# Eight sums of weight blocks from VectorE to GpSimd, the splits and gates around them reordered, and A_down by SP's plain DMAs, in a LoRA feed-forward kernel

## The chip, the cores and the metric

The kernel runs on one core of one Trainium2 chip. The metric is the device time of one execution in microseconds; several executions are timed and the median is given. All data are float32; products run on TensorE as sums of float32r parts, a high part and the remainder.

## What is computed

64 sequences of 32 rows by 512 features. Each sequence has an adapter (for the low-rank terms) and a condition (for a 32 x 32 mixing matrix).

```python
gate = x @ W_gate.T + 0.5 * (x @ A_gate[a].T) @ B_gate[a].T     # 512 -> 1376
up   = x @ W_up.T   + 0.5 * (x @ A_up[a].T)   @ B_up[a].T
act  = silu(gate) * up
h    = x + act @ W_down.T + 0.5 * (act @ A_down[a].T) @ B_down[a].T
out  = h + einsum('bct,bcd->bdt', h, W[cond])                   # mixing within a sequence
```

## The kernel before

**Tiles.** Four sequences make a tile of 128 rows; there are 16 tiles. The first stage works on pairs of tiles (8 pairs, 0 to 7, t = 0 or 1 in a pair), the down stage on one tile after the other. The 1376 features are three sections of 352, 512 and 512 columns; a unit is a section of a tile, counted k = 0 to 5 in a pair, (s, t) = (0,0), (0,1), (1,0), (1,1), (2,0), (2,1).

**Splitting.** Every float32 operand of TensorE is split: ScalarE copies it to float32r (`hi`, L500), then VectorE subtracts that from the original (`lo`, L763). B of the low-rank terms is one instruction of each (L500, L767). A product is three matmuls per slice: hi by hi, hi by lo, lo by hi.

**Fast form.** Pairs 0 and 1 are plain. From pair 2 on (`fast_pair`), the part with sections 1 and 2 is computed with seven block products and not eight, p1 to p7, as in Strassen's scheme. It needs sums of blocks of x (`sum_x`, `split_s`) and sums of weight blocks, once, for gate and up: t3 = b22 - b12, t1 = b12 - b11, t2 = b22 - t1, t4 = b21 - t2, each 128 x 1024 (`sum_weights`, L801, on VectorE during pair 1). The sums t1, t2 and t4 are written over raw weights in the landing area, which is also where the split forms of t2, t1 and t4 will lie; so each split may overwrite what another has still to read, and the waits on `w_ready` (pieces and forms whose low part is done) and `weights_summed` (sums done) in `split_forms` guard that. `t3_raw` lies under `s_hi`. The splits of these forms stand in the queues of ScalarE and VectorE by hand, in the order of `SPLITS`.

**Order on TensorE in a fast pair.** `base(pr, 0)`, `lora(pr-1, 5)`, `base(pr, 1)` with `lora(pr, 0)` in it, p1 (b11), `lora(pr, 1)`, p7 (t3; in pair 2 after p2), p2 (b21), p6 (t2), p5 (t1), p4 (t4), p3 (b22), each for gate and up. `base(pr, k)` waits until the units that used its bank are gated: in fast pairs `act_ready` must have reached 6 (pr - 1) + 4 + k. The count `act_ready` goes up when VectorE has multiplied silu(gate) by up (`gate`, L872); `turn` transposes the result to a staging area (L880), and `spill` on SP sends that to `actT_dram`, from where `load_actT` brings it back for the down stage.

**Down stage.** A tile takes 11 chunks of W_down (`down_chunks`, L1300), with the columns of A_down of the tile's adapters beside them in `wd`, so that the low-rank t comes out of the same matmuls. Within the chunks of tile m, TensorE also does `down_lora` and `mix` of tile m - 1. ScalarE and VectorE split A_down (`split_a_dn`), the activations (`split_actT`), B_down, the mixing matrix (`split_mix`) and h (`residual_h`, `split_h`) of the neighbouring tiles. GpSimd gathers B (gate and up) by indirect DMA with the row numbers of the list `rows` (L441), and in the down stage the rows of A_down (four gathers a tile), B_down and the mixing matrix. SP gathers A of gate and up with plain DMAs whose row number is loaded from `rows` into a register (`first_row`, L389).

Each queue is in order; what stands behind a waiting instruction waits too.

## Time and profile before

| | us |
|---|---|
| time, median of 3 runs | 457.99 (457.64 to 458.76) |
| the profiled execution | 457.48 |
| its span in the trace | 455.6 |
| TensorE (PE) busy | 437.4 |
| VectorE (DVE) busy | 335.0 |
| ScalarE (ACT) busy | 213.3 |
| GpSimd (POOL) busy | 168.2 |

Times in the trace count from the start of the span. The profiled execution is 1.9 us longer than its span, and 0.5 us below the median. Lines are those of the kernel before; L500, L763 and L441 are helpers that many steps share, so a step is known by its operands. In the timelines, one matmul's duration overlaps the next one's: the rate is read from the starts.

### The profile page before, as it was taken

Reading aid. Unit: us, or ns where it says so; the run is one execution under the profiler, and the core shown is the slowest. Engines: PE = TensorE matmul, PEld = TensorE weight load, DVE = VectorE, ACT = ScalarE, POOL = GpSimd, SP = SyncE. Lnnn points to the kernel's source line nnn. Section 1 sums busy time; section 2 is a strip of 40 time slices with the busy share of each in tenths; the row PEclk is TensorE's granted clock in tenths of the full one; section 3 lists DMA queues with packets and bytes.
Section 4 is the critical chain, followed back from the end, with each engine's and each line's share of the span. In section 5 each row is a group of like instructions: output and inputs, shape, how many; then the busy total and the mean of one; then the engine's idle time right before and its main releaser. Section 6 shows DMA issues by size and latency. Waiting matters only on the chain.

```text
span 455.6 us, 7248 instructions
## 1 busy us (share of the span) xinstructions
PE 437.4 (96%) x2465; PEld 393.9 (86%) x2465; DVE 335.0 (74%) x621; ACT 213.3 (47%) x396; POOL 168.2 (37%) x156
## 2 busy tenths in 40 slices
PE   5999999977999999999999999988999999999997
PEld 4978988865898888888888888988999999999996
DVE  6778698876876866967867857976766676676665
ACT  6664334365436335444444444925434545433441
POOL 3612120120311211111111551675566676665630
PEclk9999999999899999999999999999999999999999
DMA  8965663325667467466475589787556666555631
GB/s 268 378 221 150 182 181 108 104 81 147 167 170 210 109 163 193 112 199 157 112 205 148 141 260 337 196 201 201 170 173 192 205 199 202 176 175 175 201 104 46
DMA packets 99699, 81.12 MB, mean 178 GB/s; under 512 B 50928, under 2 KB 83056, under 8 KB 99664
## 3 DMA queue, kind: packets, MB, share of 16 engines
q1 hardware_dynamic: 88368, 47.27, 37.1%
q0 software_dynamic: 11008, 33.30, 24.0%
q8 instruction: 19, 0.31, 0.3%
q10 hardware_dynamic: 288, 0.10, 0.1%
q14 instruction: 16, 0.13, 0.1%
HBM read 65.18 MB, written 15.47 MB: 177 GB/s over the span
## 4 chain that ended last, share of the span: by engine, by line
PE 86%; DVE 7%; DMA 2%; ACT 2%; issue 1%; SPq 1%; DVEq 0%; ACTq 0%
PE bank L1300 24%; PE bank L1146 9%; PE bank L1147 9%; PE bank L1148 8%; PE bank L1191 8%; PE bank L1192 8%; PE bank L1193 8%; PE bank L1214 4%; PE bank L1213 4%; PE bank L1330 2%; DVE wd L763 2%; DMA actT_raw<-actT_dram 2%; PE bank L1310 1%; DVE b_gu L767 1%; PE bank L1315 1%
## 5 line engine op out<-in xcount | busy, mean ns | idle before, releaser
L441 POOL DMA_INDIRECT b_raw<-in_b_rows,rows x48 | 50.8, 1059 | 199.3 <-DVE b_gu L767 198.7
L1300 PE MATMUL bank<-wd,actT_hi 128*128 128x288 f32 x648 | 112.0, 295 | 3.1 <-DVE actT_lo L763 1.9
L1300 PEld LDWEIGHTS bank<-wd,actT_hi 128*128 128x128 f32 x648 | 95.5, 188 | 4.7 <-issue 3.5
L441 POOL DMA_INDIRECT a_dn_raw<-in_a_dn_rows,rows x64 | 75.5, 1180 | 19.5 <-issue 19.5
L767 DVE SCALAR_TENSOR_TENSOR b_gu<-b_raw,low_rows,b_gu 128x1024 fp32r<-128x1024 f32 (+1 forms) x48 | 55.6, 1159 | 30.6 <-ACT b_gu L500 30.6
L1300 PE MATMUL bank<-wd,actT_lo 128*128 128x288 f32 (+1 forms) x324 | 69.4, 296 | 0.0
L1300 PEld LDWEIGHTS bank<-wd,actT_lo 128*128 128x128 f32 (+1 forms) x324 | 51.9, 188 | 0.0
L500 ACT ACTIVATE b_gu<-b_raw 128x1024 fp32r<-128x1024 f32 (+1 forms) x48 | 46.2, 963 | 12.2 <-DMA b_raw<-in_b_rows,rows 10.7
L585 ACT ACTIVATE act<-bank 128x512 f32<-128x512 f32 (+1 forms) x48 | 26.2, 547 | 44.1 <-PE bank L1214 43.9
L763 DVE TENSOR_TENSOR actT_lo<-actT_raw,actT_hi 128x1280 fp32r<-128x1280 f32 (+1 forms) x32 | 27.0, 885 | 15.5 <-ACT actT_hi L500 14.6
L872 DVE TENSOR_TENSOR act<-act,bank 128x512 f32<-128x512 f32 (+1 forms) x48 | 29.9, 622 | 8.1 <-PE bank L1214 7.3
L1213 PE MATMUL bank<-b_gu,tT_hi 128*128 128x512 f32 (+1 forms) x96 | 35.5, 370 | 0.0
L1214 PE MATMUL bank<-b_gu,tT_lo 128*128 128x512 f32 (+1 forms) x96 | 35.5, 370 | 0.0
L880 DVE STREAM_TRANSPOSE staging<-act 128x512 f32<-128x512 f32 (+1 forms) x48 | 31.4, 654 | 3.4
L500 ACT ACTIVATE tdT_hi<-tdT_raw 128x128 fp32r<-128x128 f32 x16 | 5.0, 311 | 60.2 <-DVE tdT_raw L1050 60.2
L1146 PE MATMUL bank<-w_gate_hi,xT_hi 128*128 128x480 f32 (+2 forms) x72 | 27.0, 375 | 5.5 <-DVE w_gate_lo L763 5.5
L441 POOL DMA_INDIRECT b_dn_raw<-in_b_dn_rows,rows x16 | 18.0, 1125 | 36.7 <-PE bank L1300 26.6
L1147 PE MATMUL bank<-w_gate_lo,xT_hi 128*128 128x480 f32 (+2 forms) x72 | 26.7, 371 | 0.0
L1148 PE MATMUL bank<-w_gate_hi,xT_lo 128*128 128x480 f32 (+2 forms) x72 | 26.7, 370 | 0.0
L500 ACT ACTIVATE actT_hi<-actT_raw 128x1280 fp32r<-128x1280 f32 (+1 forms) x32 | 23.3, 775 | 2.9 <-DMA actT_raw<-actT_dram 2.9
L1146 PEld LDWEIGHTS bank<-w_gate_hi,xT_hi 128*128 128x128 f32 x72 | 14.0, 195 | 8.3 <-issue 5.2
L1146 PE MATMUL bank<-w_up_hi,xT_hi 128*128 128x352 f32 x64 | 21.2, 331 | 0.0
(177 smaller groups left out, 993.8 us busy)
## 6 DMA issues: line engine op xcount, KB each, us to landing
actT_raw<-actT_dram SPq DMA_DIRECT2D x16, 640.0 KB
actT_dram<-staging SPq DMA_DIRECT2D x64, 128.0 KB, 2.8
x_sb<-in_x SPq DMA_DIRECT2D x16, 256.0 KB, 2.9
xT_raw<-in_xT SPq DMA_DIRECT2D x15, 256.0 KB, 3.0
out<-out_sb SPq DMA_DIRECT2D x15, 256.0 KB, 2.0
a_raw<-in_a_gu_rows SPq DMA_DIRECT2D x56, 64.0 KB, 2.4
actT_dram<-staging SPq DMA_DIRECT2D x32, 88.0 KB, 3.1
wd_raw<-in_w_down SPq DMA_DIRECT2D x10, 256.0 KB, 7.1
```

Of the source, the lines that this page charges most:

```text
L441: return pool.indirect_dma_start(dst, None, src, bass.IndirectOffsetOnAxis(ap=rows[:, tile, col:col + 1], axis=0))
L500: return nc.scalar.activation(dst, src, ACT.Copy)
L767: return nc.vector.scalar_tensor_tensor(b, raw, low_rows[:, :], b.bitcast(F32), ALU.mult, ALU.subtract)
L1146: pe.matmul(out_, x_hi, hi, start=(first and k == 0), stop=False)
L1147: pe.matmul(out_, x_hi, lo, start=False, stop=False)
L1148: last = pe.matmul(out_, x_lo, hi, start=False, stop=(stops and k == KH - 1))
L1191: pe.matmul(out_, xs[0], hi, start=(first and j == 0), stop=False, skip_group_check=True)
L1192: pe.matmul(out_, xs[0], lo, start=False, stop=False, skip_group_check=True)
L1193: last = pe.matmul(out_, xs[1], hi, start=False, stop=(j == 1), skip_group_check=True)
L1213: pe.matmul(out_, tT_hi[t][:, g, :], b, start=False, stop=False, skip_group_check=True)
L1214: pe.matmul(out_, tT_lo[t][:, g, :], b, start=False, stop=True, skip_group_check=True)\
L1300: last = pe.matmul(ps_down[e][half][:, 0:HALF], a[e][0:n, c, :], wd[0:n, c, part, at:at + HALF], start=(c == 0 and i == 0), stop=(c == NC ...
```

## The change

- `sum_weights` goes from VectorE to GpSimd: in pair 1 the eight sums stand between the gathers of B, four behind the gathers of section 1, two behind each of the first gathers of section 2.
- `SPLITS` becomes t2, t1, t4, t3. In the plain pair (pair 1), both engines split t2 later, behind B of section 2, then t1 gate, and at the pair's end, behind `split_x` (and on VectorE `sum_x`), t1 up, t4 gate and t4 up. t3 is split in pair 2 between `split_b(pr, 1, 0)` and `split_s`, which waits for it. TensorE's waits for t1 and t4 go, since p7 waits for the last form.
- In all fast pairs TensorE's waits for B stand between the product and the low-rank matmuls and not ahead of the product.
- In the last pair chunks 0 to 4 of W_down are split, in three places, and not 0 to 3 in one.
- In the down stage A_down of tiles 2 to 15 is loaded by SP with plain DMAs (`load_a_dn`), each behind the `load_actT` of the same tile; GpSimd keeps those of tiles 0 and 1. The loads for tile 2 stand ahead of `spill(7, 2)`.
- Tile 1 of the down stage: `split_a_dn(1)`, `split_actT(1)` and `mask_td(0)` stand ahead of the gates of units 4 and 5 of the last pair; TensorE begins it when units 0 to 3 are gated, with the high parts of three chunks, and does `mix(0)` behind nine chunks and not seven.

```diff
-SPLITS = [(f, m) for f in ("t2", "t3", "t1", "t4") for m in MATRICES]
+SPLITS = [(f, m) for f in ("t2", "t1", "t4", "t3") for m in MATRICES]
...
+            def load_a_dn(m):
+                reached(sp, a_dn_ready, m - 1)
+                for q in range(TILE_SEQS):
+                    sp.dma_start(a_dn_raw[m % 2][:, q, :],
+                                 a_dn_rows[bass.ds(first_row(m, TILE_SEQS + 1 + q), P), :])\
+                        .then_inc(a_dn_landed[m % 2], 16)
...
             sp.wait_ge(s_used, FAST)
             load_x(0, 0)
+            load_actT(2, 0)
+            load_a_dn(2)
             load_x(1, 1)
             spill(PAIRS - 1, 2)
-            load_actT(2, 0)
             load_actT(3, 1)
+            load_a_dn(3)
...
                 load_actT(2 * j + 2, 0)
+                load_a_dn(2 * j + 2)
...
                 load_actT(2 * j + 3, 1)
+                load_a_dn(2 * j + 3)
...
-                    gather(a_dn_raw[m % 2][:, q, :], a_dn_rows, m, TILE_SEQS + 1 + q).then_inc(a_dn_landed[m % 2], 16)
+                    gather(a_dn_raw[m][:, q, :], a_dn_rows, m, TILE_SEQS + 1 + q).then_inc(a_dn_first_landed[m], 16)
+
+            def sum_weights(f, i):
+
+                if f == "t3":
+                    pool.wait_ge(w_ready, GU_PIECES)
+                elif f != "t1":
+                    pool.wait_ge(weights_summed, 4 if f == "t2" else 6)
+                a, b = {"t3": ("b22", "b12"), "t1": ("b12", "b11"), "t2": ("b22", "t1"), "t4": ("b21", "t2")}[f]
+                m = MATRICES[i]
+                nc.gpsimd.tensor_tensor(block_raw(f, m), block_raw(a, m), block_raw(b, m), ALU.subtract)\
+                    .then_inc(weights_summed, 1)
+
+            def pair_with_sums(pr):
+                gather_b(pr, 1, 0)
+                gather_b(pr, 1, 1)
+                sum_weights("t3", 0)
+                sum_weights("t3", 1)
+                sum_weights("t1", 0)
+                sum_weights("t1", 1)
+                gather_b(pr, 2, 0)
+                sum_weights("t2", 0)
+                sum_weights("t2", 1)
+                gather_b(pr, 2, 1)
+                sum_weights("t4", 0)
+                sum_weights("t4", 1)
+                gather_b(pr + 1, 0, 0)
...
-            for pr in range(PAIRS):
+            pair(0)
+            pair_with_sums(1)
+            for pr in range(PLAIN, PAIRS):
                 pair(pr)
...
             gather_b_dn(0)
             for m in range(2, TILES):
-                gather_a_dn(m)
                 pool.wait_ge(down_done, m - 1)
                 gather_b_dn(m - 1)
                 gather_mix(m - 1)
...
                     if f == "t2":
                         sc.wait_ge(w_ready, GU_PIECES)
                         sc.wait_ge(weights_summed, 6)
-                    elif f == "t1":
-                        sc.wait_ge(w_ready, GU_PIECES + i)
-                        sc.wait_ge(weights_summed, 8)
                     elif f == "t3":
                         sc.wait_ge(xT_used[1], PLAIN)
-                    else:
+                    elif m == "up":
+                        sc.wait_ge(w_ready, GU_PIECES + i - (1 if f == "t1" else 0))
+                        sc.wait_ge(weights_summed, 8)
+                    elif f == "t4":
                         sc.wait_ge(w_ready, GU_PIECES + i)
                     hi(form_part(f, m, "hi"), block_raw(f, m)).then_inc(w_hi_ready, 1)
...
                 if isinstance(pr, int) and pr == PLAIN:
-                    sc.wait_ge(w_ready, GU_PIECES + 4)
+                    sc.wait_ge(w_ready, GU_PIECES + 8)
...
                 split_a(pr + 1, 0)
                 split_a(pr + 1, 1)
-                split_forms(0, 2)
                 silu(pr, 2)
                 split_b(pr, 2, 0)
+                split_forms(0, 2)
                 split_x(pr + 1, 0)
                 silu(pr, 3)
                 split_b(pr, 2, 1)
+                split_forms(2, 3)
                 split_x(pr + 1, 1)
+                split_forms(3, 6)
...
                 split_b(pr, 0, 1)
                 silu(pr, 0)
                 split_t(pr, 1)
-                if first:
-                    split_forms(2, 4)
                 copy_p1(pr)
                 split_b(pr, 1, 0)
                 silu(pr, 1)
                 if first:
+                    split_forms(6, 8)
                     split_s(pr)
-                    split_forms(4, 6)
                     silu(pr, 2)
+                    split_b(pr, 1, 1)
                     copy_p7(pr)
-                    split_forms(6, 8)
-                    split_b(pr, 1, 1)
                 else:
                     copy_p7(pr)
                     split_b(pr, 1, 1)
                     silu(pr, 2)
...
                     split_x(pr + 1, 0)
+                else:
+                    split_down(0, 3)
...
-                    split_down(0, 4)
+                    split_down(3, 5)
...
             split_a_dn(0, 0)
             sc.wait_ge(p5_done, 2 * FAST)
             split_actT(0, 0)
-            split_down(4, NC)
-            silu(PAIRS - 1, 4)
+            split_down(5, NC)
             split_a_dn(1, 1)
-            silu(PAIRS - 1, 5)
             sc.wait_ge(s_used, FAST)
             split_actT(1, 1)
+            silu(PAIRS - 1, 4)
+            silu(PAIRS - 1, 5)
             split_b_dn(0, 0)
             split_td(0)
             split_mix(0, 0)
+            split_h(0, 0)
             split_a_dn(2, 0)
-            split_h(0, 0)
             split_actT(2, 0)
             split_b_dn(1, 1)
...
-                sum_weights("t3")
                 gating(pr, 0)
                 split_b(pr, 1, 0)
-                sum_weights("t1")
                 gating(pr, 1)
                 split_b(pr, 1, 1)
-                sum_weights("t2")
                 split_a(pr + 1, 0)
                 split_a(pr + 1, 1)
-                split_forms(0, 2)
                 gating(pr, 2)
                 split_b(pr, 2, 0)
+                split_forms(0, 2)
                 split_x(pr + 1, 0)
                 gating(pr, 3)
-                sum_weights("t4")
                 split_b(pr, 2, 1)
+                split_forms(2, 3)
                 split_x(pr + 1, 1)
                 sum_x(pr + 1)
+                split_forms(3, 6)
...
                 split_b(pr, 0, 1)
-                if first:
-                    split_forms(2, 4)
                 split_b(pr, 1, 0)
                 if first:
+                    split_forms(6, 8)
                     split_s(pr)
                 gating(pr, 1)
-                if first:
-                    split_forms(4, 6)
-                else:
-                    split_b(pr, 1, 1)
+                split_b(pr, 1, 1)
                 gate(pr, 2)
+                if last:
+                    split_down(0, 1)
                 add_u3(pr, 0)
-                if not first:
-                    turn(pr, 2)
+                turn(pr, 2)
                 add_u3(pr, 1)
-                if first:
-                    turn(pr, 2)
-                    split_forms(6, 8)
-                    split_b(pr, 1, 1)
                 if not last:
                     split_x(pr + 1, 0)
+                else:
+                    split_down(1, 2)
                 add_u7(pr, 0)
+                if last:
+                    split_down(2, 3)
                 add_u7(pr, 1)
                 split_b(pr, 2, 0)
                 if not last:
                     split_a(pr + 1, 0)
                     split_a(pr + 1, 1)
                 else:
-                    split_down(0, 4)
+                    split_down(3, 5)
                 gating(pr, 3)
...
             split_a_dn(0, 0)
             split_actT(0, 0)
-            split_down(4, NC)
+            split_down(5, NC)
+            split_a_dn(1, 1)
+            split_actT(1, 1)
+            split_b_dn(0, 0)
+            mask_td(0, 0)
             gating(PAIRS - 1, 4)
-            split_a_dn(1, 1)
             gating(PAIRS - 1, 5)
-            split_actT(1, 1)
-            ve.wait_ge(s_used, FAST)
-            split_b_dn(0, 0)
-            down(1, 1)
+            split_mix(0, 0)
+            residual_h(0, 0)
+            split_a_dn(2, 0)
+            split_actT(2, 0)
+            split_b_dn(1, 1)
+            residual_out(0, 0)
...
                 for i, m in enumerate(MATRICES):
-                    pe.wait_ge(w_ready, GU_PIECES + 3 + i)
+                    pe.wait_ge(w_ready, GU_PIECES + 7 + i)
...
                     p7(pr)
-                pe.wait_ge(b_ready[0], NS * pr + 2)
                 for i, m in enumerate(MATRICES):
                     pe.wait_ge(p1_copied, fast(pr, i))
                     p2 = product(ps[m][0][:, :], xT_hi[0], xT_lo[0], 1, "b21", m, False)
                     if i:
                         p2.then_inc(xT_used[0], 1)
+                    else:
+                        pe.wait_ge(b_ready[0], NS * pr + 2)
                     lora_half(ps[m][0][:, :], 0, i, PIECE)
...
-                    pe.wait_ge(w_ready, GU_PIECES + 5 + i)
                     pe.wait_ge(u3_ready, fast(pr, i))
                     product(ps[m][3][:, :], s_hi[1], s_lo[1], 1, "t1", m, False).then_inc(p5_done, 1)
-                pe.wait_ge(b_ready[1], NS * pr + 2)
                 for i, m in enumerate(MATRICES):
-                    pe.wait_ge(w_ready, GU_PIECES + 7 + i)
                     p4 = product(ps[m][0][:, :], xT_hi[1], xT_lo[1], 1, "t4", m, False)
                     if i:
                         p4.then_inc(xT_used[1], 1)
+                    else:
+                        pe.wait_ge(b_ready[1], NS * pr + 2)
                     lora_half(ps[m][0][:, :], 1, i, PIECE)
...
-            def first_chunks(c1):
+            def first_chunks(m, e, c1):
+                pe.wait_ge(actT_hi_ready, m + 1)
                 for c in range(c1):
-                    pe.wait_ge(w_ready, DN_FIRST + c + 1)
+                    if m == 0:
+                        pe.wait_ge(w_ready, DN_FIRST + c + 1)
                     for part in range(2):
                         for half in range(2):
-                            at = half * HALF
-                            pe.matmul(ps_down[0][half][:, 0:HALF], actT_hi[0][:, c, :], wd[:, c, part, at:at + HALF],
+                            at = RR * e + half * HALF
+                            pe.matmul(ps_down[e][half][:, 0:HALF], actT_hi[e][:, c, :], wd[:, c, part, at:at + HALF],
                                       start=(c == 0 and part == 0), stop=False)
-                pe.wait_ge(actT_ready, 1)
+                pe.wait_ge(actT_ready, m + 1)
...
-            def down(m, e, first=False):
+            def down(m, e, early=False):
                 pe.wait_ge(a_dn_ready, m + 1)
-                if first:
-                    pe.wait_ge(actT_hi_ready, 1)
-                    first_chunks(3)
+                if early:
+                    first_chunks(m, e, 3)
                 else:
                     pe.wait_ge(actT_ready, m + 1)
                     reached(pe, h_ready, 2 * (m - 1))
                     down_chunks(m, e, 0, 3)
-                if not first:
+                if not isinstance(m, int) or m > 0:
                     down_lora(m - 1, 1 - e)
-                down_chunks(m, e, 3, 7)
-                if not first:
+                mix_at = 9 if early else 7
+                down_chunks(m, e, 3, mix_at)
+                if not isinstance(m, int) or m > 0:
                     reached(pe, out_ready, m - 1)
                     mix(m - 1)
-                down_chunks(m, e, 7, NC).then_inc(down_done, 1)
+                down_chunks(m, e, mix_at, NC).then_inc(down_done, 1)
 
             pe.wait_ge(act_ready, NU * (PAIRS - 1) + 2)
-            down(0, 0, first=True)
-            pe.wait_ge(act_ready, NU * PAIRS)
-            down(1, 1)
+            down(0, 0, early=True)
+            pe.wait_ge(act_ready, NU * (PAIRS - 1) + 4)
+            down(1, 1, early=True)
```

## Rows read from the trace of the kernel before

**Rows 1.** The page, part 1: busy us of each engine, share of the span, instructions.
```profile
PE 437.4 (96%) x2465; PEld 393.9 (86%) x2465; DVE 335.0 (74%) x621; ACT 213.3 (47%) x396; POOL 168.2 (37%) x156
```

**Rows 2.** Waits of TensorE over the span: waiter, releaser, us in total, times, longest.
```profile
PE bank L1191 <- DVE b_gu L767: 5.7, 2, 3.4
PE bank L1146 <- DVE w_gate_lo L763: 5.5, 2, 5.3
PE bank L1300 <- DVE actT_lo L763: 1.9, 1, 1.9
PE bank L1300 <- issue: 1.2, 1, 1.2
```

**Rows 3.** Timeline of TensorE, pair 2: start, duration, instruction, [idle time before, releaser].
```profile
87.37 0.38 PE L1146 MATMUL bank<-w_gate_hi,xT_hi 128*128 128x480 f32 x1
...
92.57 0.39 PE L1191 MATMUL bank<-b_gate_hi,xT_hi 128*128 128x512 f32 x1
...
98.44 0.50 PE L1191 MATMUL bank<-b_gate_hi,xT_hi 128*128 128x512 f32 x1 [2.31 <-DVE b_gu L767]
...
102.20 0.39 PE L1191 MATMUL bank<-t_gate_hi,s_hi 128*128 128x512 f32 x1
...
113.96 0.61 PE L1191 MATMUL bank<-t_gate_hi,xT_hi 128*128 128x512 f32 x1 [3.43 <-DVE b_gu L767]
...
119.33 0.40 PE L1191 MATMUL bank<-b_gate_hi,s_hi 128*128 128x512 f32 x1
```

**Rows 4.** Timeline of VectorE, pairs 1 and 2, same columns.
```profile
56.91 2.35 DVE L801 TENSOR_TENSOR t_raw<-gu_landing 128x1024 f32<-128x1024 f32 x2
...
81.96 0.69 DVE L763 TENSOR_TENSOR xT_lo<-xT_raw,xT_hi 128x512 fp32r<-128x512 f32 x1 [0.80 <-ACT xT_hi L500]
...
84.48 0.68 DVE L872 TENSOR_TENSOR act<-act,bank 128x512 f32<-128x512 f32 x1
...
91.08 0.48 DVE L872 TENSOR_TENSOR act<-act,bank 128x352 f32<-128x352 f32 x1
...
97.11 1.28 DVE L767 SCALAR_TENSOR_TENSOR b_gu<-b_raw,low_rows,b_gu 128x1024 fp32r<-128x1024 f32 x1 [1.48 <-ACT b_gu L500]
...
100.79 1.18 DVE L763 TENSOR_TENSOR t_gate_lo<-gu_landing,t_gate_hi 128x1024 fp32r<-128x1024 f32 x1
...
103.10 1.23 DVE L763 TENSOR_TENSOR t_up_lo<-gu_landing,t_up_hi 128x1024 fp32r<-128x1024 f32 x1 [1.13 <-ACT t_up_hi L500]
```

**Rows 5.** Timeline of ScalarE, pair 2.
```profile
96.03 1.05 ACT L500 ACTIVATE b_gu<-b_raw 128x1024 fp32r<-128x1024 f32 x1
...
97.31 1.15 ACT L500 ACTIVATE s_hi<-xT_raw 128x512 fp32r<-128x512 f32 x2
...
102.01 1.06 ACT L500 ACTIVATE t_up_hi<-gu_landing 128x1024 fp32r<-128x1024 f32 x1 [2.60 <-DVE t_gate_lo L763]
```

**Rows 6.** Timeline of GpSimd, pair 1 and start of the down stage.
```profile
55.48 0.94 POOL L441 DMA_INDIRECT b_raw<-in_b_rows,rows  x1 [3.18 <-DVE b_gu L767]
...
61.78 1.68 POOL L441 DMA_INDIRECT b_raw<-in_b_rows,rows  x1 [5.36 <-DVE b_gu L767]
...
291.54 4.11 POOL L441 DMA_INDIRECT a_dn_raw<-in_a_dn_rows,rows  x1 [0.31 <-issue]
```

**Rows 7.** DMA issues: out<-in, queue, operation, count, median us to landing.
```profile
b_raw<-in_b_rows,rows POOLq DMA_INDIRECT x48, 4.5
```

**Rows 8.** Timeline of VectorE, start of the down stage.
```profile
290.54 4.29 DVE L763 TENSOR_TENSOR wd<-wd_raw,wd 128x512 fp32r<-128x512 f32 x7
...
298.35 1.65 DVE L763 TENSOR_TENSOR actT_lo<-actT_raw,actT_hi 128x1280 fp32r<-128x1280 f32 x2
...
309.71 1.69 DVE L763 TENSOR_TENSOR actT_lo<-actT_raw,actT_hi 128x1280 fp32r<-128x1280 f32 x2 [3.94 <-ACT actT_hi L500]
```

**Rows 9.** Timeline of ScalarE: its wait for actT of tile 2.
```profile
308.20 1.47 ACT L500 ACTIVATE actT_hi<-actT_raw 128x1280 fp32r<-128x1280 f32 x2 [2.93 <-DMA actT_raw<-actT_dram]
```

**Rows 10.** Timeline of SP's queue: the issue of that load.
```profile
300.85 0.42 SPq L373 DMA_DIRECT2D actT_raw<-actT_dram  x1
```

43 lines of the change are left out of this document (18 added, 25 removed).

## The prediction

> **What bounds the kernel now.** I read the page's busy shares first: TensorE is busy for 437.4 of 455.6 us [rows 1], so nothing counts that doesn't shorten its 18 idle us or its slow stretches. The list of TensorE's waits says where these are [rows 2]: 5.5 us at the start, which the change doesn't touch; 5.7 us in two waits for `b_gu` at L1191; 1.9 and 1.2 us at L1300, ahead of the second and third tile of the down stage. From about 311 us to the end TensorE never waits, so work taken there from GpSimd, ScalarE or VectorE is worth nothing by itself.
>
> Then the timelines. The two `b_gu` waits lie in the first fast pair (pair 2): 2.31 us ahead of 98.44 and 3.43 us ahead of 113.96 [rows 3]. After the second the clock is at its lower level (1.2 of 2.4 GHz): 5.37 us pass between 113.96 and 119.33 for 16 matmuls that need 0.23 us each at the upper level, 3.7 us, so this wait costs 1.7 us more. After the 2.31 us wait the matmuls keep their rate. Together, the place costs 7.4 us, and the down stage 3.1.
>
> **Part 1: eight sums leave VectorE.** They took 1.17 us each there (the pair of 2.35 us at 56.91 and three like it), 9.4 us, all between 56.9 and 80 us [rows 4]. TensorE doesn't wait there, so their removal alone gains nothing; it makes room for splitting the forms earlier. What counts is where these splits now stand. In the plain pair both queues get `t2` and the first of `t1`, and then, behind `split_x` and `sum_x`, the three splits t1 up, t4 gate, t4 up. Each of the latter overwrites the landing area that the one before still reads, so ScalarE waits for VectorE's previous part and VectorE for ScalarE's. The same ping-pong is in the rows: t1 gate 100.79, ScalarE at 102.01 for 1.06 us, t1 up 103.10 [rows 4, 5], a period of 2.31 us.
>
> The end of the ping-pong follows. `xT_lo` at 81.96 is timed by TensorE's use of `xT` (ScalarE sits behind it), `sum_x` follows, and at 84.48 VectorE is free; there the old kernel gates unit 4 [rows 4]. Now three splits come first: 84.48 + 2.31 + 2.31 + 1.15 = 90.25, and the gate's product is there at 90.93. But TensorE wants it at 87.37, since `base(2, 1)` waits for `act_ready` 11 (the bank that unit 4 of the pair before leaves) [rows 3]. **New wait: 3.6 us**, where the old kernel had none. Queued behind it on TensorE is all of the pair; on ScalarE `silu` 4, `split_b` and `split_t` stand behind the splits. A wait of 3.43 us was followed by the lower clock, so I charge 1.7 us for this one too.
>
> From there: the old kernel took 5.20 us from 87.37 to the first product of the fast form at 92.57; now 91.0 + 5.2 + 1.7 = 97.9 (at the upper clock, VectorE's gate of unit 0, 91.08 + 0.48 shifted by 5.77, would hold it to 97.4, so the clock costs 0.5 here). At 98.44 the wait for `b_gu` stood ahead of the product of b21, 5.87 us after 92.57; now one product of six matmuls (1.4) goes ahead of it, and 1.4 of its 2.45 us are gained, 1.0 stays. Next late is `s_ready`: `t3` is split last, after `split_b`, and `split_s` needs both parts, because `s_hi` lies over `t3_raw`. Counted from the start of p1: ScalarE's `split_b` at 3.46, `silu` and two forms to 6.8; VectorE's `b_gu` at 4.54, then 1.2 each for it and t3 gate, which begins at 5.85, and t3 up, to 8.2; ScalarE's `s_hi` 1.15, VectorE's `s_lo` 1.3 (two of the 0.69 of `xT_lo`, overlapped): 10.7 [rows 3 to 5]. TensorE would be there at 9.63 - 1.4 = 8.2: **a wait of 2.4 us**, where `s_ready` had been hidden. So p7 begins at 97.9 + 10.7 = 108.6 and not at 102.20. Then three steps of 12 matmuls (8.2 us) and, since the splits of `t4` are long done, p4 without its 3.43 us and at the upper clock: 108.6 + 8.2 + 3.7 = 120.5 against 119.33. **The place costs 1.2 us more than before, even if GpSimd is free of charge.** The gain goes to the two new waits.
>
> **Part 2: the sums on GpSimd.** The trace has no arithmetic of GpSimd. The bounds for one sum: below, VectorE's 1.17; above, the longest GpSimd row, 4.11 (a gather) [rows 6]. I take 2.35, twice VectorE's, nearer to the row of the same operation. GpSimd is free for them after its gather at 55.48 + 0.95, thus from 56.7: eight sums 18.8, two gathers 2.5, all done by 78.0. They are first wanted when ScalarE comes to t1 up, at 81.9. So at 2.35 they are hidden, and up to 2.8 us each. What they delay are the gathers of `b_raw` queued behind: 61.78 becomes 66.2, landing 4.5 us later at 71 [rows 6, 7], when ScalarE is just at it; hidden.
>
> That holds if the engines don't disturb each other. The rows say they do. The gather at 61.78 takes 1.68 us instead of 0.95 while VectorE runs a sum; the one at 291.54 takes 4.11 and ends 0.95 after seven back-to-back subtractions of VectorE do (290.54 + 4.29 = 294.83) [rows 6, 8]. So a GpSimd instruction waits for VectorE's with two SBUF inputs. The gather reads only a list of rows; whether VectorE waits in turn for an instruction of GpSimd that reads all the time, no row shows. The Trainium skill, "SBUF — State Buffer", § Who interferes with whom, says so: a VectorE instruction with two SBUF inputs contends with one of GpSimd that reads SBUF, for an exclusive lock, held for the whole instruction. By that rule the change loses, by its absence the estimate above stands. "GPSIMD Engine Reference" of the Trainium skill, § 3.1, has 4497 ns for 2048 elements, which makes 2.25 us an estimate for one sum here; the sum below would be 0.1 us lower per sum.
>
> I walk it through with 2.35 (starts of whoever comes first, each waiting for the other). VectorE's instructions with two SBUF inputs up to the last sum: four `b_gu` of 1.2, two `split_a` of 0.6, `t2` twice 1.15, `xT_lo` 0.6, together 8.9 us. GpSimd never rests from 56.7 on, so each of them adds itself to its chain: 78.0 + 8.9, less what TensorE's timing puts behind it. If VectorE always goes first, the last sum ends at 87.8; if they alternate, at 82.5, but then `t2`, `xT_lo` and the gate of unit 3 are late and TensorE waits 3 us at `base(2, 0)`; if GpSimd goes first, at 78.3, with VectorE's backlog behind it. The three orders put the gate of unit 4 at 95.4, 96.2 and 94.3 instead of 90.25. I take 95.4: **5.1 us more**, all on the path, since TensorE is waiting for it.
>
> **Part 3: down stage.** `split_actT(1)` now stands ahead of units 4 and 5 on both engines. VectorE: splits of wd from 290.54 (one chunk fewer, 293.4), then `a_dn` 0.85 and actT 1.6, done at 296; TensorE comes at 298.2 (1.9 us before the old actT part was done, 298.35 + 1.65, and 0.1 of signal) [rows 2, 8]. The 1.9 us go, and the gates of 4 and 5, now behind `mask_td(0, 0)`, are next: 298.6 + 1.3 + 2.7 = 302.6, and mix(0), which needs what follows, moves two chunks back (9 for 7) and is wanted at 305.9 (a chunk takes 0.8 us: tile 1 ran from 300.1 to 310.2, where the third tile began its wait of 1.2, and held 11 chunks and some 1.3 us of lora and mix); `h_lo` is ready at 305.8. No cover is left there: a delay of VectorE goes to TensorE in full. The 1.2 us come from actT of tile 2, issued at 300.85 and landed by 308.20 [rows 9, 10]. Its load now stands ahead of `spill(7, 2)`, goes out when tile 0 is split (289.8) and lands by 298. Next late is VectorE: after `h_lo` 305.8, `a_dn` 0.85, actT 1.7 (the row at 309.71) [rows 8]: 308.5, against TensorE at 308.4. **Gain 1.9 + 1.2 - 0.1 = 3.0 us.**
>
> The loads of `A_down` on SP: four more issues of about 0.4 us a tile, behind `load_actT(m)` and ahead of the `store`'s wait, in time that SP waits away; wanted a tile later. Costed at nothing; without that cover 1.6 us a tile at most, and the same bytes move. GpSimd gives up 56 gathers; TensorE doesn't wait for any. `split_down` between `add_u3` and `add_u7` fills pauses of 0.6 us; nothing. The moved waits for `b_ready` in later pairs gain nothing, as there TensorE doesn't wait [rows 2].
>
> **Sum and rivals** (the profiled run is 457.48, 0.5 below the median of 457.99; differences are laid on the median).
> - Forecast, locked both ways: +1.2 + 5.1 - 3.0 = +3.3, 461.3 us; own range 459.5 to 464 (sums of 1.8 to 3 us, order of grants). Chance 0.5.
> - Faster: no mutual blocking. One mechanism, sums hidden behind TensorE's work up to 81.9; decides if the eighth is done by then. +1.2 - 3.0 = -1.8, 456.2 us. For it: all VectorE rows keep their length beside gathers. Chance 0.27.
> - One way: GpSimd waits for VectorE, not the reverse, as far as rows show it. Sums end at 78.0 + 7.7 = 85.7, t1 up follows, the gate of unit 4 comes at 92.6: +2.3 more, +0.5, 458.5 us. Chance 0.18.
> - The change doesn't do what it says: the loads from SP come late and ScalarE, waiting at `split_a_dn`, holds up `split_h`: against it speaks that an issue takes SP 0.42 us [rows 10], so eight or so leave most of a tile's 10 us free. It would cost up to 1.6 us a tile, 14 tiles. Chance 0.05.
>
> A measurement can tell some 0.3% (1.4 us) here: faster is below 456.6, slower above 459.4. Faster gets the first rival's 0.27 and a little of the one-way case, same 0.2 most of the one-way case and the high end of the first rival, slower the locked case and the late loads, some 0.5. The range takes in the first two rivals (the first less 1.2 for the clock and its own roundings) and the upper bound of the walk: 455.0 to 464.0.
>
> **What would show it.** A TensorE wait before L1146 (`base(2, 1)`) for `act` L872 of 3.6 us in the mild case and 8 or more in the locked one; a wait for `s_lo` before p7; none before p4. VectorE's subtractions and `b_gu` longer than their 1.15 and 1.28 us between 57 and 85, or unchanged. The 1.9 and 1.2 us gone. Wrong would make me: sums well under 1.8 us, or the gate of unit 4 much before 90.

## The result, and the profile after

| | before | changed |
|---|---|---|
| median of 4 runs | 458.13 us (457.64 to 458.76) | 467.79 us (467.11 to 468.91) |
| span of the profiled execution | 455.6 us | 465.8 us |
| mean granted clock of TensorE | 0.996 | 0.985 |

The changed kernel is slower: ratio 1.0212, 95% interval 1.0188 to 1.0236. The forecast was 461.3 with a range up to 464.0. The sign was right; the loss is three times what was forecast.

Part 1 of the page, three engines of the changed kernel (busy us, share of the span, instructions), beside [rows 1]:

```profile
PE 442.1 (95%) x2465; PEld 397.0 (85%) x2465; DVE 342.9 (74%) x613; ACT 213.4 (46%) x396; POOL 116.6 (25%) x108
```

GpSimd fell to 116.6 us on the same line and TensorE rose by 4.7, though it does the same 2465 matmuls: a part of them ran at the lower clock. The waits of TensorE in the changed kernel (waiter, releaser, us in total, times, longest), to be read against [rows 2]:

```profile
PE bank L1175 <- DVE w_gate_lo L806: 6.5, 2, 5.5
PE bank L1175 <- DVE act L904: 6.0, 2, 5.2
PE bank L1242 <- DVE tT_lo L806: 3.0, 1, 3.0
PE bank L1220 <- DVE s_lo L806: 2.4, 1, 2.4
PE bank L1242 <- DVE b_gu L810: 1.6, 2, 0.9
PE bank L1345 <- DVE h_lo L806: 1.3, 1, 1.3
```

Of the old waits past the start, the 5.7 us for `b_gu` have become 1.6, and the 1.9 and 1.2 us at the down stage one of 1.3. New are 5.2 for `act`, 3.0 for `tT_lo` and 2.4 for `s_lo`. Where they lie is in the timeline of TensorE (start, duration, instruction, wait before it and its releaser; L1175 is the old L1146, L1220 the old L1191):

```profile
34.20 0.50 PE L1175 MATMUL bank<-t_gate_hi,xT_hi 128*128 128x512 f32 x1 [0.76 <-DVE act L904]
...
66.26 0.40 PE L1242 MATMUL bank<-b_gu,tT_hi 128*128 128x352 f32 x1 [2.96 <-DVE tT_lo L806]
...
98.42 0.74 PE L1175 MATMUL bank<-w_gate_hi,xT_hi 128*128 128x480 f32 x1 [5.20 <-DVE act L904]
...
106.39 0.40 PE L1220 MATMUL bank<-b_gate_hi,xT_hi 128*128 128x512 f32 x1
...
112.24 0.50 PE L1242 MATMUL bank<-b_gu,tT_hi 128*128 128x512 f32 x1 [0.94 <-DVE b_gu L810]
...
117.17 0.50 PE L1220 MATMUL bank<-t_gate_hi,s_hi 128*128 128x512 f32 x1 [2.37 <-DVE s_lo L806]
...
121.62 0.40 PE L1220 MATMUL bank<-t_gate_hi,s_hi 128*128 128x512 f32 x1
...
130.70 0.39 PE L1220 MATMUL bank<-b_gate_hi,s_hi 128*128 128x512 f32 x1
...
143.20 0.43 PE L1242 MATMUL bank<-b_gu,tT_hi 128*128 128x352 f32 x1 [0.66 <-DVE b_gu L810]
...
328.19 0.47 PE L1345 MATMUL bank<-h_hi,mix_hi 128*128 128x512 f32 x1 [1.28 <-DVE h_lo L806]
```

The 5.20 us at 98.42 are the wait that was forecast at `base(2, 1)`, with 3.6 us if the engines don't disturb each other and over 8 if they do. The 0.94 are the rest of the `b_gu` wait, the 2.37 the forecast wait for `s_lo`. Three were not forecast: 2.96 us for `tT_lo` in pair 1, 0.66 in pair 3, 1.28 in tile 2 of the down stage. And the clock is low longer. From the first matmul of `base(2, 1)` to the first of p1 pass 7.97 us against 5.20 in [rows 3], from p7 to p6 4.45 instead of 2.72. One window of the changed kernel, and the same one of the kernel before (stretch, its length, busy us of TensorE and instructions, granted clock, DMA share, GB/s), have the clock at 0.66 and at 1.00:

```profile
99.00:107.00 8.00, 8.00 (x31) 0.66 0.25 66
```

```profile
99.00:107.00 8.00, 8.00 (x37) 1.00 0.76 205
```

In the kernel before, the clock is at 1.00 at `base(2, 1)` too (87 to 93 us).

What VectorE and GpSimd do at 56 to 83 us, in their timelines:

```profile
56.43 4.75 POOL L477 TENSOR_TENSOR t_raw<-gu_landing 128x1024 f32<-128x1024 f32 x2
61.14 4.68 POOL L477 TENSOR_TENSOR gu_landing<-gu_landing 128x1024 f32<-128x1024 f32 x2
...
69.59 4.76 POOL L477 TENSOR_TENSOR gu_landing<-gu_landing 128x1024 f32<-128x1024 f32 x2
...
76.89 4.76 POOL L477 TENSOR_TENSOR gu_landing<-gu_landing 128x1024 f32<-128x1024 f32 x2
```

```profile
56.76 9.35 DVE L806 TENSOR_TENSOR tT_lo<-tT_raw,tT_hi 128x256 fp32r<-128x256 f32 x1 [0.48 <-ACT tT_hi L539]
...
69.36 6.08 DVE L810 SCALAR_TENSOR_TENSOR b_gu<-b_raw,low_rows,b_gu 128x1024 fp32r<-128x1024 f32 x1
...
77.98 4.76 DVE L810 SCALAR_TENSOR_TENSOR b_gu<-b_raw,low_rows,b_gu 128x1024 fp32r<-128x1024 f32 x1
...
97.59 0.68 DVE L904 TENSOR_TENSOR act<-act,bank 128x512 f32<-128x512 f32 x1
```

A sum takes GpSimd 2.35 us, as I took it. The subtraction `tT_lo`, 0.43 us in e1 below, takes 9.35: it begins 0.33 us after the first sum and ends at 66.1, 0.3 us behind the fourth. Two `b_gu` of 1.2 us take 6.08 and 4.76. The last line is the gate of unit 4, which stood at 84.48 in [rows 4].

**The account.** To compare places I count from the wait of 0.8 us for `act` near 34 us (33.33 before, 34.20 in the changed kernel), which lies ahead of anything the change touches. The start differs by 0.9 us. From there to p3 the changed kernel takes 130.70 - 34.20 = 96.5 us against 86.0 [rows 3]: 10.5 more. Pair 3 costs 1.0 more, the down stage gives back 2.2: 0.9 + 10.5 + 1.0 - 2.2 = 10.2, the difference of the spans.

### The profile page after: what moved, and what is told of

Read it like the earlier page. It is cut to its first block, busy times and chain, and to the rows that moved or that the text cites. A ratio compares the mean times of both kernels' runs of the same rounds, so it can differ in the third digit from the quotient of the medians.

```text
span 465.8 us, 7499 instructions
## 1 busy us (share of the span) xinstructions
PE 442.1 (95%) x2465; PEld 397.0 (85%) x2465; DVE 342.9 (74%) x613; ACT 213.4 (46%) x396; POOL 116.6 (25%) x108
## 4 chain that ended last, share of the span: by engine, by line
PE 72%; DVE 12%; issue 6%; DMA 3%; ACT 3%; SPq 3%; POOL 1%; DVEq 0%; ACTq 0%
PE bank L1330 25%; PE bank L1220 7%; PE bank L1221 7%; PE bank L1222 7%; PE bank L1175 5%; PE bank L1177 5%; PE bank L1176 5%; PE bank L1242 3%; PE bank L1243 3%; DVE b_gu L810 3%; PE bank L1360 2%; DVE act L904 2%; DMA b_raw<-in_b_rows,rows 1%; PE bank L1340 1%; DVE t_gate_lo L806 1%
## 5 line engine op out<-in xcount | busy, mean ns | idle before, releaser
L1330 PE MATMUL bank<-wd,actT_hi 128*128 128x288 f32 (+1 forms) x636 | 109.9, 295 | 0.0
L453 POOL DMA_INDIRECT b_raw<-in_b_rows,rows x48 | 49.8, 1038 | 191.8 <-DVE b_gu L810 191.2
L1330 PEld LDWEIGHTS bank<-wd,actT_hi 128*128 128x128 f32 (+1 forms) x636 | 93.8, 189 | 1.4 <-issue 0.2
L810 DVE SCALAR_TENSOR_TENSOR b_gu<-b_raw,low_rows,b_gu 128x1024 fp32r<-128x1024 f32 (+1 forms) x48 | 63.9, 1332 | 30.9 <-ACT b_gu L539 30.8
L1330 PE MATMUL bank<-wd,actT_lo 128*128 128x288 f32 (+1 forms) x318 | 68.1, 296 | 0.0
L453 POOL DMA_INDIRECT b_dn_raw<-in_b_dn_rows,rows x16 | 15.4, 965 | 122.0 <-PE bank L1330 111.9
L1175 PE MATMUL bank<-w_gate_hi,xT_hi 128*128 128x480 f32 (+2 forms) x72 | 28.1, 390 | 11.8 <-DVE w_gate_lo L806 6.5
L1176 PE MATMUL bank<-w_gate_lo,xT_hi 128*128 128x480 f32 (+2 forms) x72 | 27.7, 384 | 0.0
L1175 PEld LDWEIGHTS bank<-w_gate_hi,xT_hi 128*128 128x128 f32 x72 | 14.6, 202 | 15.1 <-issue 11.0
L1242 PEld LDWEIGHTS bank<-b_gu,tT_hi 128*128 128x128 f32 x96 | 18.3, 191 | 8.4 <-issue 3.4
L539 ACT ACTIVATE h_hi<-x_sb 128x224 fp32r<-128x224 f32 (+1 forms) x30 | 11.1, 414 | 22.7 <-DVE x_sb L1092 22.7
```

The source lines that it names most:

```text
L453: return pool.indirect_dma_start(dst, None, src, bass.IndirectOffsetOnAxis(ap=rows[:, tile, col:col + 1], axis=0))
L539: return nc.scalar.activation(dst, src, ACT.Copy)
L810: return nc.vector.scalar_tensor_tensor(b, raw, low_rows[:, :], b.bitcast(F32), ALU.mult, ALU.subtract)
L1175: pe.matmul(out_, x_hi, hi, start=(first and k == 0), stop=False)
L1176: pe.matmul(out_, x_hi, lo, start=False, stop=False)
L1242: pe.matmul(out_, tT_hi[t][:, g, :], b, start=False, stop=False, skip_group_check=True)
```

## The experiments

All times are medians beside runs of the kernel before on the same chip, with the ratio to it and its 95% interval.

### The orders without GpSimd, and GpSimd without the orders

`e1_sums_back` is the changed kernel with the sums where they had been:

```diff
-            pair(0)
-            pair_with_sums(1)
-            for pr in range(PLAIN, PAIRS):
+            for pr in range(PAIRS):
                 pair(pr)
...
                 split_t(pr, 1)
+                sum_weights("t3")
                 gating(pr, 0)
                 split_b(pr, 1, 0)
+                sum_weights("t1")
```

> The changed kernel with the eight sums back on VectorE at their old places; all other orders, waits and loads as changed. Theory L (a GpSimd instruction with SBUF inputs and a VectorE instruction with two SBUF inputs exclude each other, and a run of GpSimd sums keeps VectorE out to its end): VectorE's longest instruction falls from 9.35 us to about 1.3, the 3.0 us wait for tT_lo is gone, the wait for the gate of unit 4 ahead of base(2, 1) falls from 5.2 to about 4 us; total 457 to 458.5 us. Rival R (the new orders cost the time, GpSimd's sums are harmless): 463 us or more, and the wait ahead of base(2, 1) stays at 5 us.

Measured: 462.83 us, ratio 1.0105 (1.0038 to 1.0172), span 460.4. TensorE in pair 2:

```profile
92.82 0.74 PE L1161 MATMUL bank<-w_gate_hi,xT_hi 128*128 128x480 f32 x1 [3.86 <-DVE act L886]
...
100.76 0.39 PE L1206 MATMUL bank<-b_gate_hi,xT_hi 128*128 128x512 f32 x1
...
111.58 0.50 PE L1206 MATMUL bank<-t_gate_hi,s_hi 128*128 128x512 f32 x1 [2.38 <-DVE s_lo L777]
...
116.01 0.39 PE L1206 MATMUL bank<-t_gate_hi,s_hi 128*128 128x512 f32 x1
```

No wait for `tT_lo`. To p3 (125.08, with the mark at 34.77) it takes 4.3 us more than the kernel before. So the orders by themselves cost 4.3 us, where I had 1.2, and the sums another 6.2, where I had 5.1.

`e2_only_sums` is the reverse: the kernel before, and only `sum_weights` moved to GpSimd, among its gathers as in the change.

> The kernel before with nothing changed but the eight sums, which go to GpSimd between the gathers of pair 1, as in the changed kernel. Theory L: VectorE's tT_lo is stretched to 9 us beside the run of four sums, TensorE waits 3 us at lora(1, 1) and some 3 us or more later in pair 2: 463 to 467 us. Rival R: VectorE gets 9.4 us of room and TensorE's waits stay as they were: 457 to 459 us.

Measured: 469.33 us, ratio 1.0255 (1.0202 to 1.0308). Its waits of TensorE that the kernel before lacks:

```profile
66.60 0.40 PE L1227 MATMUL bank<-b_gu,tT_hi 128*128 128x352 f32 x1 [3.72 <-DVE tT_lo L792]
...
84.88 0.80 PE L1160 MATMUL bank<-t_gate_hi,xT_hi 128*128 128x512 f32 x1 [3.06 <-DVE act L890]
```

VectorE has `tT_lo` here at 9.62 us. The sums alone cost 11 us here, more than beside the other orders of the change (5 us between the medians of e1 and the changed kernel); they are its dearest single edit.

### What of a sum is it that VectorE waits for?

Two kernels keep the place and number of the GpSimd instructions and change their kind; both leave the subtraction of the weight blocks out:

```diff
-                nc.gpsimd.tensor_tensor(block_raw(f, m), block_raw(a, m), block_raw(b, m), ALU.subtract)\
-                    .then_inc(weights_summed, 1)
+                nc.gpsimd.memset(block_raw(f, m), 1.0).then_inc(weights_summed, 1)
```

in `e7_memsets`, and `nc.gpsimd.tensor_copy(block_raw(f, m), block_raw(a, m)).then_inc(weights_summed, 1)` in `e7_copies`.

> The changed kernel with a memset of the same block on GpSimd in place of each sum; the weight sums are left out, so the sections from pair 2 on are computed from wrong blocks. A memset writes SBUF and reads nothing. Theory L (what excludes each other is the reading of SBUF through a path that VectorE's second input shares): VectorE's tT_lo keeps its 0.43 us and b_gu its 1.25; no wait for tT_lo; total 460 to 462.5 us, as with the sums on VectorE. Rival (any GpSimd instruction on SBUF blocks VectorE): tT_lo is lengthened to the end of the run of memsets.

> The changed kernel with a copy of the first block on GpSimd in place of each sum; the subtraction is left out, so the sections from pair 2 on are computed from wrong blocks. A copy reads one operand in SBUF and writes one. Theory L: beside the copies tT_lo is lengthened, to the end of the run of four if the run is not broken, by some 4 us if a copy takes about 1.1 us. Rival (only GpSimd instructions with two SBUF inputs block): tT_lo keeps its 0.43 us.

Measured: 463.32 and 462.35 us, one run each, beside 458.85. GpSimd and VectorE with memsets:

```profile
58.69 1.87 POOL L477 MEMSET t_raw<- 128x1024 f32 x2
...
59.12 0.43 DVE L805 TENSOR_TENSOR tT_lo<-tT_raw,tT_hi 128x256 fp32r<-128x256 f32 x1 [0.48 <-ACT tT_hi L538]
```

and with copies:

```profile
57.42 2.03 POOL L477 COPY t_raw<-gu_landing 128x1024 f32<-128x1024 f32 x2
59.39 2.02 POOL L477 COPY gu_landing<-gu_landing 128x1024 f32<-128x1024 f32 x2
...
57.56 4.13 DVE L805 TENSOR_TENSOR tT_lo<-tT_raw,tT_hi 128x256 fp32r<-128x256 f32 x1 [0.49 <-issue]
```

Beside memsets, which read no SBUF, `tT_lo` keeps its 0.43 us. Beside copies it takes 4.13 and ends at 61.7, 0.3 us behind the fourth copy. So it is the reading of GpSimd that VectorE's instruction with two SBUF inputs waits for. The Trainium skill, "SBUF — State Buffer", § Who interferes with whom, states just that. It calls the pair of ports that the two engines share an exclusive lock and says, of VectorE's modes that use both ports, that whoever issues first holds it for the whole instruction. The traces agree on the kind; on the length they show more, four instructions and not one. Both kernels take the time of e1 within what a single run can tell (462.83). TensorE doesn't wait for `tT_lo` in either, and it waits 3.61 us at `base(2, 1)` in both, no more than the 3.86 of e1: eight GpSimd instructions of 1 us at this place are affordable, eight of 2.35 are not.

### Is it the one long wait?

`e3_sums_after_t` lets GpSimd begin behind `tT_lo`; `e6_each_waits` lets each sum wait for the completion of the one before, so that they are no uninterrupted run:

```diff
                 if f == "t3":
                     pool.wait_ge(w_ready, GU_PIECES)
+                    pool.wait_ge(tT_ready[1], 2)
```

```diff
                 m = MATRICES[i]
+                done = 2 * ("t3", "t1", "t2", "t4").index(f) + i
+                if done:
+                    pool.wait_ge(weights_summed, done)
```

> The changed kernel with one more wait on GpSimd: the first sum starts only when tT_lo of tile 1 of pair 1 is done. Theory L: the 3.0 us wait at lora(1, 1) and the low clock behind it (1.5 us) go, the sums start 0.7 us later, b_gu of section 1 is now the one that waits for the run of sums; since TensorE wants it 5 us later than tT_lo, it costs less: 463 to 465 us. Rival (which instruction meets the run makes no difference, VectorE's total is what counts): 467 to 468 us, as changed.

> The changed kernel, but each sum on GpSimd first waits for the completion of the one before (by the semaphore weights_summed). Theory H (GpSimd keeps VectorE out as long as its instructions follow each other without a pause): every sum now ends with a pause, VectorE comes in after at most one sum, so tT_lo at 57 us lasts 2.5 to 3 us and not 9.4, the 3.0 us wait at lora(1, 1) goes, total 463 to 465.5 us. Rival (VectorE gets in only when GpSimd has nothing left in its queue, or the pause is too short): tT_lo stays at 9 us or more, total 467 to 469 us.

Measured: 465.36 us, ratio 1.0169 (1.0135 to 1.0203), and 466.16, ratio 1.0188 (1.0144 to 1.0231). VectorE's `tT_lo` in the one and in the other, and GpSimd's first sums of the latter:

```profile
57.53 0.43 DVE L807 TENSOR_TENSOR tT_lo<-tT_raw,tT_hi 128x256 fp32r<-128x256 f32 x1 [0.48 <-issue]
```

```profile
57.38 2.51 DVE L809 TENSOR_TENSOR tT_lo<-tT_raw,tT_hi 128x256 fp32r<-128x256 f32 x1 [0.48 <-issue]
...
57.18 4.96 POOL L480 TENSOR_TENSOR t_raw<-gu_landing 128x1024 f32<-128x1024 f32 x2
62.22 5.74 POOL L480 TENSOR_TENSOR gu_landing<-gu_landing 128x1024 f32<-128x1024 f32 x2
```

TensorE no longer waits for `tT_lo` in either, and yet little is won: the wait at `base(2, 1)` grows from 5.20 to 6.37 and 6.38 us, with 1.9 and 0.8 us at 85 us besides. Now the engines take turns: a pair of sums takes up to 6.08 us instead of 4.75, and an instruction of VectorE waits for about one sum. The long wait for `tT_lo` is thus one form of the cost and not its cause; the cause is that 18.8 us of sums share one resource with VectorE's two-input work while that work is wanted.

### The order of the three splits

`e11_gate_first` is e1 with the three form splits behind silu and gating of unit 4:

```diff
                 split_x(pr + 1, 1)
-                split_forms(3, 6)
...
                 silu(pr - 1, 4)
+                if first:
+                    split_forms(3, 6)
```

(on VectorE the same, behind `gating(pr - 1, 4)`).

> The kernel of e1_sums_back (all orders of the change, sums on VectorE) with the three form splits that the change put ahead of the gating of unit 4 (t of block 1 up, t of block 4 gate, t of block 4 up) put behind silu and gating of unit 4. Theory: the wait of 3.86 us at the base product of (2,1) goes, but tT_lo of block 1 up is then late for its LoRA product: a wait of about 4.4 us there or a little after takes its place, so the time stays within about 1 us of e1 (462.8, ratio about 1.010). Rival: the wait at (2,1) and the low clock behind it go and nothing comes in their place: 462.8 - 3.9 - 1.0 = 457.9, ratio 1.000.

Measured: 462.42 us, ratio 1.0089 (1.0061 to 1.0117).

```profile
95.50 0.63 PE L1230 MATMUL bank<-b_gu,tT_hi 128*128 128x352 f32 x1 [4.66 <-DVE tT_lo L778]
...
111.51 0.80 PE L1208 MATMUL bank<-t_gate_hi,s_hi 128*128 128x512 f32 x1 [2.35 <-DVE s_lo L778]
```

The wait at `base(2, 1)` is gone, and one of 4.66 us for `tT_lo` stands in its place a few microseconds later. The 4 us aren't the price of the place ahead of the gate but of three chained splits, 2.3 us each, at a point where VectorE has no time to spare. Where they stood before, inside pair 2, they made `b_gu` late and cost the 3.43 us of [rows 3]; with B split ahead of them (e8 below) this wait is gone.

### The down stage

`e4_down_only` is the kernel before with the down-stage part of the change (orders, tile 1 begun early, A_down by SP), `e10_sp_only` the kernel before with the loads of A_down alone:

```diff
             load_actT(2, 0)
+            load_a_dn(2)
             load_actT(3, 1)
+            load_a_dn(3)
...
             for m in range(2, TILES):
-                gather_a_dn(m)
```

> The kernel before with the down-stage part of the change alone (A_down from tile 2 on by SP, the new order of tile 1 on all engines, W_down's splits in the last pair). By the prediction's sum: 3.0 us faster, 455.1. By what the changed kernel's trace shows (waits of 1.9 and 1.2 us gone, a new one of 1.3 us for h_lo in tile 2): 1.8 to 2.1 us faster, 456.1. Rival: the loads on SP cost in every tile of the down stage: 458 us or more.

> The kernel before, with only A_down of the tiles 2 to 15 loaded by plain DMAs of SP with a row number from a register, everything else as before (sums on VectorE, order of the down stage as before). Theory: the way in which A_down is loaded is worth nothing by itself: the ratio is 1.000 within 0.3%, with at most one new wait of about 1.2 us for h_lo in tile 2 (SP's load of a_dn(3) stands behind the spill of (7,2)); the gain of e4_down_only (about 2 us) is that of the order of the forms before the down stage. Rival: the gathers of GpSimd held the waits of 1.9 and 1.2 us at the start of the down stage, so they go with the gathers: about 455.5, ratio 0.995. Second rival: SP pays for each tile (register arithmetic, queue) and the time is over before by 0.5 us or more in the 14 tiles outside of any wait of tile 2.

Measured: 456.48 us for e4, ratio 0.9961 (0.9931 to 0.9991), and 463.97 for e10, ratio 1.0128 (1.0088 to 1.0168). In e4 the waits of 1.9 and 1.2 us are gone and one of 1.21 us for `h_lo` in tile 2 has come. In e10 the 1.9 us for `actT_lo` have stayed; the gain is that of the orders. The loads by themselves lose 5 us, which neither theory had. SP, ScalarE and TensorE of e10 show where:

```profile
303.39 3.68 SPq L396 DMA_DIRECT2D a_dn_raw<-in_a_dn_rows  x4
```

```profile
308.61 0.79 ACT L510 ACTIVATE wd<-a_dn_raw 128x704 fp32r<-128x704 f32 x1 [5.72 <-DMA a_dn_raw<-in_a_dn_rows]
```

```profile
312.10 0.48 PE L1328 MATMUL bank<-h_hi,mix_hi 128*128 128x512 f32 x1 [3.61 <-DVE h_lo L776]
```

SP comes to the loads of tile 2 at 303.39, behind the spill and the load of actT. In the kernel before GpSimd issued these gathers between 290.15 and 298.16 (one of the four is in [rows 6]). ScalarE waits 5.72 us for them, and TensorE, in tile 1, 3.61 for `h_lo`, since the split of A_down stands ahead of that of h; behind it the clock is low for some 3 us. From tile 3 on the two kernels run alike, 9.92 us a tile in both. So a load by SP costs nothing in itself; its place in SP's queue costs. In the changed kernel the same place holds the load for tile 3:

```profile
314.80 1.98 SPq L343 DMA_DIRECT2D actT_dram<-staging  x4
...
318.90 3.66 SPq L396 DMA_DIRECT2D a_dn_raw<-in_a_dn_rows  x4
```

```profile
324.64 0.79 ACT L539 ACTIVATE wd<-a_dn_raw 128x704 fp32r<-128x704 f32 x1 [1.20 <-DMA a_dn_raw<-in_a_dn_rows]
```

`spill(7, 2)` at 314.80 waits for the gate of unit 5, which the change has put later. The load stands behind it, and the four issues take 3.66 us, 0.9 each and not the 0.42 of [rows 10]. The kernel before had that price on show: its eight loads of A with a row number from a register, from 104.50 on, take SP 8.58 us.

### A version that beats both

`e8_best` takes the kernel before, the down-stage part with `load_a_dn(3)` ahead of `spill(7, 2)`, the waits for B behind the first product, and in pair 2 puts `split_b(pr, 1, 1)` and then the splits of t4 earlier, with the sums left on VectorE:

```diff
                 gate(pr, 2)
+                if first:
+                    split_b(pr, 1, 1)
+                    split_forms(6, 7)
                 add_u3(pr, 0)
...
-                    split_forms(6, 8)
-                    split_b(pr, 1, 1)
+                    split_forms(7, 8)
```

`e9_a_first` adds this, from pair 2 on:

```diff
+                if a_first and not last:
+                    load_a(pr + 1, 0)
+                    load_a(pr + 1, 1)
                 if not last:
                     load_xT(pr + 1, 0)
                     load_xT(pr + 1, 1)
                 if not first:
                     spill(pr - 1, 2)
-                if not last:
+                if not a_first:
                     load_a(pr + 1, 0)
                     load_a(pr + 1, 1)
```

`e12_best_with_sums` is e9 with the sums on GpSimd.

> The kernel before with the down-stage part of the change, A_down of tile 3 loaded ahead of the last spill, the waits for B moved behind the first product, and in pair 2 the B of section 1 split ahead of the forms of t4, of which one is split ahead of add_u3 and one behind it; the sums stay on VectorE. The sum of the parts: 2.2 us for the down stage and 1.2 for the wait for h_lo, 1.4 for b21's product ahead of the wait, 3.4 for the wait ahead of p4 and 1.7 for the low clock behind it: 9.5 us or so faster, 448 to 450.5 us. Rival (VectorE has no room left in pair 2, and the waits only move): 453 us or more.

> The kernel of e8_best, with SP's loads of a(g) ahead of those of xT(g) from pair 2 on. Theory: what is left in e8's pair 3 (TensorE's waits of 1.78 and 1.13 us) comes from ScalarE's waits of 3.20 and 4.30 us for a_raw, whose loads stand in SP's queue behind the loads of xT, and these behind their own wait. With a ahead both waits of TensorE go and none of over 0.5 us takes their place in pair 3: e8's 453.0 - 2.9 = about 450.1, ratio to before about 0.981. Rival: the transfers share the same 16 DMA engines, so xT comes later by what a comes earlier, and TensorE waits for xT instead: 452 to 454, no change against e8.

> The kernel of e9_a_first with one edit: the eight sums go to GpSimd, placed among its gathers as in the change. Theory: the sums cost what e2_only_sums showed with the order of before (a wait for tT_lo of about 3.7 us at 66, one for the gate of unit 3 of about 3 us at 85, and the lower clock behind each, 11 us in all), since nothing in e9 alters pair 1: 449.2 + 11 = about 460, ratio about 1.003. Rival: the cost is that of the order of the change with which the sums were tried (about 5 us between e1_sums_back and the changed kernel), as the later splits take the delay up: 454 to 455, ratio about 0.99. Second rival: with the best order the sums cost nothing, 449.

Measured: e8 453.03 us, ratio 0.9874 (0.9857 to 0.9891); e9 449.22, ratio 0.9794 (0.9760 to 0.9829), 9.5 us under the kernel before; e12 458.47, ratio 1.0003 (0.9974 to 1.0031). All waits of TensorE in e9 past the start, but two of under 0.4 us:

```profile
PE bank L1241 <- DVE b_gu L787: 0.9, 1, 0.9
PE bank L1174 <- DVE act L892: 0.7, 1, 0.7
PE bank L1219 <- DVE bank L860: 0.6, 1, 0.6
```

e8 fell short of what I expected by two waits, 1.78 and 1.13 us in pair 3. They came from ScalarE's waits of 3.20 and 4.30 us for `a_raw`, whose loads stood behind those of xT. With `a` first both are gone, and 3.8 us of the medians with them (3.2 of the spans). e12 shows the cost of the sums once more, in the best order known:

```profile
65.97 0.40 PE L1255 MATMUL bank<-b_gu,tT_hi 128*128 128x352 f32 x1 [3.02 <-DVE tT_lo L812]
...
84.23 0.79 PE L1188 MATMUL bank<-t_gate_hi,xT_hi 128*128 128x512 f32 x1 [3.06 <-DVE act L910]
```

3.0 and 3.1 us of waits, and 8.4 us of span in all (456.5 against 448.1).

## Why the prediction was off

**Right, with their sizes.** One sum takes 2.35 us. The wait at `base(2, 1)` was to be 3.6 us without GpSimd and was 3.86 (e1); the rest of the `b_gu` wait 1.0, measured 0.94; the wait for `s_lo` 2.4, measured 2.38; none before p4. The 1.9 and 1.2 us at the down stage went. The two engines block each other both ways, the likeliest case: `tT_lo` at 9.35 us rules out the one-way case and the free one, and the pairs of sums at 5.74 and 6.08 us in e6 show that GpSimd waits too.

**Wrong step 1, the clock.** In "so I charge 1.7 us for this one too" the term was mis-sized, and left out once. Behind the wait at `base(2, 1)` the lower clock cost 7.94 - 5.20 = 2.7 us (e1), since the matmuls of the base product follow at 0.40 us apart, and not 0.22, until 97.4. Behind the wait for `s_lo` p7 took 4.43 us and not 2.72, 1.7 us more that I hadn't charged: I had gone by the 2.31 us of [rows 3], which none followed. With 0.3 us of wait and small change these are the 3.1 us by which p3 came later than I had it.

Neither number is a fixed price, though. Behind the same wait of 3.61 us at `base(2, 1)` the way to p1 took 1.4 us more than the 5.20 in e7_copies and 2.8 more in e7_memsets. And in e6 the clock stayed up behind the same wait for `s_lo`:

```profile
114.06 0.49 PE L1223 MATMUL bank<-t_gate_hi,s_hi 128*128 128x512 f32 x1 [2.35 <-DVE s_lo L809]
...
116.92 0.39 PE L1223 MATMUL bank<-t_gate_hi,s_hi 128*128 128x512 f32 x1
...
131.44 0.45 PE L1178 MATMUL bank<-w_gate_hi,xT_hi 128*128 128x480 f32 x1 [1.66 <-DVE act L907]
...
140.88 0.43 PE L1245 MATMUL bank<-b_gu,tT_hi 128*128 128x352 f32 x1 [1.17 <-DVE b_gu L813]
```

There p7 takes 2.86 us, but TensorE then waits 1.66 and 1.17 us in pair 3, where the changed kernel waits 0.66 (e7_copies does as e6: 1.39 and 1.14). From p7 to pair 4, e6 takes 0.8 us more than the changed kernel, not 1.7 less. So the lower clock took its 1.7 us at that place, but the end of pair 3 was set by something else, SP's queue (below).

**Wrong step 2, the walk through the lock.** Its list of VectorE's two-input instructions began with `b_gu` and left out `tT_lo` of block 1, the very first and the only one that TensorE was waiting for. It also let each instruction wait for one sum; `tT_lo` waited for four. TensorE lost 4.8 us there, 2.96 of wait and 1.9 at the lower clock, in a pair where I had written that it doesn't wait. GpSimd had gone first, which is the third of the walk's orders and not the one I took. The wait at `base(2, 1)`, which the walk had at 3.6 + 5.1 = 8.7 us, was 5.20. The gate of unit 4 came at 97.6 (walk: 95.4), but not since the sums ended late: the last ended at 81.65, and I had 87.8 (which doesn't follow from the walk's own terms, 78.0 + 8.9 = 86.9). Mostly, what came late was TensorE's own use of `xT`, delayed by the 4.8 us: ScalarE's `xT_hi` at 86.98 waited 3.33 us for it. The rest is VectorE's backlog:

```profile
89.25 0.68 DVE L806 TENSOR_TENSOR xT_lo<-xT_raw,xT_hi 128x512 fp32r<-128x512 f32 x1
```

`xT_lo` begins 1.6 us behind the end of `xT_hi`, in e1 0.3; that is the 1.3 us between the waits of 3.86 and 5.20. The sum, 4.8 + 1.4 = 6.2 against 5.1, was nearly right by a way that was mostly wrong: that is luck. One reading was off too: the gather at 291.54 ends 0.82 us behind VectorE's seventh subtraction and not 0.95.

**Wrong step 3, A_down.** The loads were "wanted a tile later" and "Costed at nothing": those of tile 3 came late. The load stood behind a spill whose gate the same change had moved. It is the rival to which I gave 0.05, in one tile and not in fourteen. Of the forecast 3.0 us 2.2 remained (e4 has the same 2.2: a span of 454.0 against 455.6, with a start 0.6 later); in e8, e9 and e12, with this load ahead of the spill, TensorE doesn't wait for `h_lo`. The sentence before, that no cover is left in this place, should have made me look.

**Not looked at: pair 3.** SP's load of xT for pair 3 waits for `s_ready`, and the spill and the loads of `a` stand behind it. With `s_ready` later (xT goes out at 99.82 before, at 117.15 in the changed kernel), ScalarE waits 3.34 and 3.80 us for `a_raw`, and TensorE 0.66 for `b_gu`: 1.0 us. That this chain, and not the clock, sets the end of pair 3 is what e6 shows above; with the loads of `a` ahead (e9) both its waits are gone. A queue with a wait in it hands a delay on to all loads behind it; I had followed TensorE, VectorE and ScalarE past the new wait, and not SP.

The sum of the steps, place by place: 3.1 + 1.1 + 0.8 + 1.0, and 0.9 by which the start differed (it differs by up to 1.7 us between executions of kernels that are alike there: the mark lay between 33.33 and 34.98). Together 6.9, the distance from 3.3 to 10.2.

**Open.** What decides whether GpSimd keeps the resource through several of its queued instructions (changed kernel, e2, e7_copies, e12) or takes turns with VectorE (e3, e6). In e3 the first four sums are as much an uninterrupted run as in the changed kernel, and `b_gu` got in after one. Open too is what decides whether the lower clock follows a wait, and for how long.
